# Two alternating sums in DRAM for the first experts' scatter-adds, joined where the projection and the attention load rows

## The reference

```python
x = x + 0.5 * ffn(layernorm(x))
x = x + attn(layernorm(x))
x = x + 0.5 * ffn(layernorm(x))
```

## Time and profile before

| | |
|---|---|
| time, median of 3 runs | 1454.43 us (1454.4 to 1458.55) |
| time of the profiled execution | 1453.73 us |
| its span, first to last instruction | 1452.5 us |
| PE busy | 1225.6 us, 84% |
| DVE busy | 908.8 us, 63% |
| ACT busy | 661.8 us, 46% |
| POOL busy | 531.1 us, 37% |
| mean granted TensorE clock | 0.945 of full speed |
| q0 (software) | 53.49 MB, 18.1% of 16 engines |
| q1 (hardware) | 47.17 MB, 9.4% of 16 engines |

### The profile page before, as it was taken

The page is one execution under the profiler, slowest core; times in us unless marked ns, Lnnn a source line. Parts: engine busy times, 40 slices in busy tenths (PEclk is TensorE's granted clock), DMA queues, the critical chain, the costliest instruction groups (busy, mean ns, idle before and its releaser), DMA issues.

```text
span 1452.5 us, 22060 instructions
## 1 busy us (share of the span) xinstructions
PE 1225.6 (84%) x7484; PEld 781.7 (54%) x7484; DVE 908.8 (63%) x2063; ACT 661.8 (46%) x1313; POOL 531.1 (37%) x423
## 2 busy tenths in 40 slices
PE   3278888865989899999999999999999717998985
PEld 3266666644877554455445455444433316776763
DVE  7865665545999564666576766667620485665653
ACT  2424444432645653555355555455567332443442
POOL 4424444434000110001424553626358362544443
PEclk9689999997999999999999999989999958999998
DMA  9654555443111000000000004010000342555444
GB/s 341 256 167 88 90 97 90 88 71 94 35 32 28 31 31 2 31 31 31 0 31 31 2 1 146 1 59 2 2 30 1 126 174 51 89 94 91 93 88 65
DMA packets 50827, 102.06 MB, mean 70 GB/s; under 512 B 7104, under 2 KB 16576, under 8 KB 50624
## 3 DMA queue, kind: packets, MB, share of 16 engines
q0 software_dynamic: 20928, 53.49, 18.1%
q1 hardware_dynamic: 29792, 47.17, 9.4%
HBM read 67.35 MB, written 38.01 MB: 73 GB/s over the span
## 4 chain that ended last, share of the span: by engine, by line
PE 49%; DMA 25%; DVE 16%; issue 6%; ACT 3%; POOL 0%; SPq 0%; POOLq 0%; DVEq 0%; ACTq 0%
DMA x<-Y,DI 12%; DMA out<-Y,DI 11%; PE bank L1372 9%; PE bank L1384 9%; PE bank L877 8%; PE bank L1397 5%; PE bank L1434 3%; DVE PM L890 3%; PE bank L1202 3%; PE bank L716 2%; DVE bank L892 2%; DMA XG<-xn,TK 2%; PE bank L646 1%; PE bank L739 1%; PE bank L1414 1%
## 5 line engine op out<-in xcount | busy, mean ns | idle before, releaser
L1476 ACT ACTIVATE P<-bank 128x512 f32<-128x512 f32 (+3 forms) x640 | 305.7, 535 | 299.2 <-PE bank L1372 295.3
L890 DVE TENSOR_REDUCE PM<-bank 128x1 f32<-128x512 f32 x384 | 252.8, 685 | 102.2 <-PE bank L877 101.2
L1372 PE MATMUL bank<-Qs,Ks 98*128 98x512 f32 (+3 forms) x640 | 248.3, 412 | 7.9 <-ACT P L1476 6.3
L877 PE MATMUL bank<-Ks,Qs 96*128 96x512 f32 (+3 forms) x640 | 238.1, 391 | 7.3 <-DVE PM L890 4.5
L1372 PEld LDWEIGHTS bank<-Qs,Ks 98*128 98x128 f32 x640 | 117.2, 190 | 151.9 <-issue 85.6
L1515 POOL TENSOR_SCALAR_AFFINE_SELECT P<-P 128x512 f32<-128x512 f32 x64 | 41.2, 644 | 429.3 <-ACT P L1476 290.3
L1530 POOL TENSOR_TENSOR CH<-CH,P 128x512 f32<-128x512 f32 x128 | 160.2, 1281 | 72.3 <-ACT P L1476 71.4
L892 DVE CUSTOM_DVE_ANT_0 bank<-bank,KB 128x128 f32<-128x128 f32 (+3 forms) x256 | 124.8, 497 | 57.9 <-PE bank L877 57.1
L877 PEld LDWEIGHTS bank<-Ks,Qs 96*128 96x128 f32 x640 | 121.8, 191 | 60.7 <-DVE PM L890 31.3
L1384 PE MATMUL bank<-P,V 128*32 128x512 f32 (+3 forms) x1280 | 153.4, 551 | 0.2 <-POOL P L1515 0.2
L827 DVE TENSOR_TENSOR DL<-W,DH 128x512 fp32r<-128x512 f32 x152 | 98.3, 688 | 51.4 <-ACT DH L788 51.4
(11 more groups left out here) (167 smaller groups left out, 1893.7 us busy)
## 6 DMA issues: line engine op xcount, KB each, us to landing
xn<-XN SPq DMA_DIRECT2D x8, 1024.0 KB, 7.0
WR<-L_ffn_w POOLq DMA_DIRECT2D x16, 512.0 KB, 13.8
WR<-L_ffn_w SPq DMA_DIRECT2D x16, 512.0 KB, 7.9
W<-L_ffn_w POOLq DMA_DIRECT2D x8, 512.0 KB, 24.0
XA<-x SPq DMA_DIRECT2D x16, 256.0 KB, 2.7
XO<-x SPq DMA_DIRECT2D x4, 1024.0 KB, 5.4
out<-XO SPq DMA_DIRECT2D x4, 1024.0 KB, 4.4
W<-L_ffn_w SPq DMA_DIRECT2D x8, 512.0 KB, 7.4
```

The costliest lines, as they stand in the source:

```text
L877: pe.matmul(bk(g, bank)[:, 0:n], g.Qs[b][0:96, G % 4 * 4 + h, c * P:c * P + P], g.Ks[0:96, G % 4, k * BQ:k * BQ + n], start=True, stop=Tru ...
L890: dve.tensor_reduce(dst, bk(g, bank)[:, 0:n], AX.X, ALU.max).then_inc(s(f"free{bank}"), 1)
L1372: pe.matmul(bk(g, i % 3)[:, o:BQ], g.Ks[0:98, G % 4, k * P:k * P + P], g.Qs[G // 4][0:98, G % 4 * 4 + j, o:BQ], start=True, stop=True).the ...
L1476: act.activation(a.P4[buffer_of(n)][:, j, o:BQ], bk(g, i % 3)[:, o:BQ], ACT.Exp, scale=scale).then_inc(s("exp"), 1)
```

## The change

The first experts get a second sum, `x1b`, filled with zeros; even tiles add into `x1` and odd tiles into `x1b`. A scatter-add waits for the one two tiles before it instead of the one before. The readers of the sum load the rows of `x1` as before, and POOL then issues a DMA with accumulation that adds the rows of `x1b` on top in SBUF. For the second experts the list of sums has one member, so their waits are those of before. The core of the diff:

```diff
+def added(g, f, j):
+    n = len(g.acc[f])
+    return g.s(f"add{f}_{j % n}"), 16 * (j // n + 1)
+
+def all_added(g, f, wait):
+    for j in range(NJ - len(g.acc[f]), NJ):
+        wait(*added(g, f, j))
...
             pool.wait_ge(s("y"), b + j)
-            if j == 1:
-                before_adding()
+            if j - 1 < len(acc):
+                before_adding(j - 1)
             else:
-                pool.wait_ge(s(f"add{f}"), 16 * (j - 1))
+                pool.wait_ge(*added(g, f, j - 1 - len(acc)))
             pool.indirect_dma_start(
-                out=acc[:, :], ...
+                out=acc[(j - 1) % len(acc)][:, :], ...
...
     def weigh(j):
         if j >= 3:
-            dve.wait_ge(s(f"add{f}"), 16 * (j - 2))
+            dve.wait_ge(*added(g, f, j - 3))
...
 def sp_start_sums(g):
     for q in range(4):
-        sp.dma_start(g.x1[512 * q:512 * q + 512, :], x[512 * q:512 * q + 512, :]).then_inc(s("acc"), 16)
-    sp.dma_start(g.x1[T:T + P, :], zero).then_inc(s("dump"), 16)
+        sp.dma_start(g.x1[512 * q:512 * q + 512, :], x[512 * q:512 * q + 512, :]).then_inc(s("acc0"), 16)
+    sp.dma_start(g.x1[T:T + P, :], zero).then_inc(s("acc0"), 16)
+    for q in range(4):
+        sp.dma_start(g.x1b[512 * q:512 * q + 512, :].rearrange("(i p) d -> i p d", p=P),
+                     zero.unsqueeze(0).to_broadcast([4, P, D])).then_inc(s("acc1"), 16)
+    sp.dma_start(g.x1b[T:T + P, :], zero).then_inc(s("acc1"), 16)
     sp.dma_start(g.out[T:T + P, :], zero).then_inc(s("dump"), 16)
...
 def pool_project(g):
+    def second(i):
+        pool.wait_ge(s(f"xa{i % 3}"), 16 * (i // 3 + 1))
+        pool.dma_start(p.X[:, i % 3, :], g.x1b[i * P:i * P + P, :], accum_op=ALU.add).then_inc(s(f"xb{i % 3}"), 16)
+
+    for i in range(3):
+        second(i)
     pool.memset(g.Ks[96:98, :, :].bitcast(F32), 1.0).then_inc(s("kone"), 1)
...
+    for i in range(3, NT):
+        second(i)
...
     def norm(i):
-        dve.wait_ge(s(f"xa{b}"), 16 * (i // 3 + 1))
+        dve.wait_ge(s(f"xb{b}"), 16 * (i // 3 + 1))
...
-                        put(at + 6, ("xo", G0 // 4))
+                        put(at + 2, ("xo", G0 // 4))
+                        put(at + 7, ("xob", G0 // 4))
                         put(at + 9, ("finish", G0 // 4))
...
+        elif step[0] == "xob":
+            b = step[1]
+            pool.wait_ge(s("xo"), 16 * b + 16)
+            pool.dma_start(a.XO[:], g.x1b[BQ * b:BQ * b + BQ, :].rearrange("(i p) d -> p i d", p=P),
+                           accum_op=ALU.add).then_inc(s("xob"), 16)
...
         if c == 0:
-            dve.wait_ge(s("xo"), 16 * b + 16)
+            dve.wait_ge(s("xob"), 16 * b + 16)
...
+        def sum_started(j):
+            pool.wait_ge(s(f"acc{j}"), 80)
```

More of the change, by code:

```diff
@@ L648, in pe_route, with pool_experts @@
     ins.then_inc(s(f"slots{f}"), 1)
-def pool_experts(g, f, acc, before_adding):
+def added(g, f, j):
[4 more added lines that the diff above has]
+        wait(*added(g, f, j))
+def pool_experts(g, f, before_adding):
     s, pool, r, x = g.s, g.nc.gpsimd, g.r[f], g.x[f]
-    b = f * NJ
+    b, acc = f * NJ, g.acc[f]
     def gather(j):
@@ L675, in pool_experts @@
             pool.wait_ge(s("y"), b + j)
-            if j == 1:
-                before_adding()
+            if j - 1 < len(acc):
+                before_adding(j - 1)
             else:
-                pool.wait_ge(s(f"add{f}"), 16 * (j - 1))
+                pool.wait_ge(*added(g, f, j - 1 - len(acc)))
             pool.indirect_dma_start(
-                out=acc[:, :], out_offset=bass.IndirectOffsetOnAxis(ap=r.DI[:, j - 1:j], axis=0),
-                in_=x.Y[:, (j - 1) % 3, :], in_offset=None, compute_op=ALU.add).then_inc(s(f"add{f}"), 16)
+                out=acc[(j - 1) % len(acc)][:, :], out_offset=bass.IndirectOffsetOnAxis(ap=r.DI[:, j - 1:j], axis=0),
+                in_=x.Y[:, (j - 1) % 3, :], in_offset=None, compute_op=ALU.add).then_inc(added(g, f, j - 1)[0], 16)
 def pe_experts(g, f):
@@ L1001, in sp_project @@
     s, sp, d, p = g.s, g.nc.sync, g.d, g.p
-    sp.wait_ge(s("add0"), 16 * NJ)
+    all_added(g, 0, sp.wait_ge)
     def load(i):
@@ L1022, in pool_project @@
     s, pool, p = g.s, g.nc.gpsimd, g.p
-    pool.wait_ge(s("add0"), 16 * NJ)
+    all_added(g, 0, pool.wait_ge)
+    def second(i):
[3 more added lines that the diff above has]
+        second(i)
     pool.memset(g.Ks[96:98, :, :].bitcast(F32), 1.0).then_inc(s("kone"), 1)
@@ L1037, in dve_project @@
     hd = lambda ap: ap.rearrange("p (h d) -> p h d", d=HD)
-    dve.wait_ge(s("add0"), 16 * NJ)
+    all_added(g, 0, dve.wait_ge)
     def norm(i):
         b = i % 3
-        dve.wait_ge(s(f"xa{b}"), 16 * (i // 3 + 1))
+        dve.wait_ge(s(f"xb{b}"), 16 * (i // 3 + 1))
         dve.bn_stats(p.st[:], p.X[:, b, :]).then_inc(dv.sem, 1)
@@ L1106, in act_project @@
     act.activation(g.NM[:, 0:1], g.Kc[:, C_ID:C_ID + 1], ACT.Sqrt)
-    act.wait_ge(s("add0"), 16 * NJ)
+    all_added(g, 0, act.wait_ge)
     def root(i):
@@ L1331, in attend_plan @@
     assert not later and not extra and not ahead, (later, extra, len(ahead))
-    plan += [("weigh", len(TILES) - 1), ("out", 15), ("xo", 3), ("up1", 4), ("tsum", 15), ("even", 15)]
+    plan += [("weigh", len(TILES) - 1), ("out", 15), ("xo", 3), ("xob", 3), ("up1", 4), ("tsum", 15), ("even", 15)]
     for c in range(6):
@@ L1552, in add, with proj_added @@
         if c == 0:
-            dve.wait_ge(s("xo"), 16 * b + 16)
+            dve.wait_ge(s("xob"), 16 * b + 16)
         dve.tensor_tensor(a.XO[:, c, :], bk(g, bank), a.XO[:, c, :], ALU.add).then_inc(s(f"free{bank}"), 1)
-    def added(b, c):
+    def proj_added(b, c):
         bank, use = g.ring.where[("proj", b, c)]
@@ L1595, in dve_attend @@
         elif kind == "stats":
-            added(step[1], step[2])
+            proj_added(step[1], step[2])
             dve_stats(g, g.R1, a.XO, step[2])
@@ L1604, in dve_attend @@
             c = step[1]
-            added(3, c)
+            proj_added(3, c)
             dve_stats(g, g.R1, a.XO, c)
@@ L1673, in build @@
         g.x1 = nc.dram_tensor("x1", [T + P, D], F32, kind="Internal").ap()
+        g.x1b = nc.dram_tensor("x1b", [T + P, D], F32, kind="Internal").ap()
+        g.acc = [(g.x1, g.x1b), (out,)]
         g.md = [nc.dram_tensor(f"top_{G}", [8, BQ], F32, kind="Internal").ap() for G in range(4 * NB)]
@@ L1705, in build @@
         sp_start_sums(g)
[L1707 to L1711, removed]
+        def sum_started(j):
+            pool.wait_ge(s(f"acc{j}"), 80)
+        pool_experts(g, 0, sum_started)
         pe_experts(g, 0)
@@ L1717, in build @@
         pool_project(g)
-        pe.wait_ge(s("add0"), 16 * NJ)
+        all_added(g, 0, pe.wait_ge)
         pe_project(g)
@@ L1739, in build, with residual_stored @@
         sp_down1(g)
-        def residual_stored():
+        def residual_stored(j):
             pool.wait_ge(s("stored"), 64)
-        pool_experts(g, 1, out, residual_stored)
+            pool.wait_ge(s("dump"), 16)
+        pool_experts(g, 1, residual_stored)
         pe_experts(g, 1)
@@ L1747, in build @@
         dve_experts(g, 1)
-        sp.wait_ge(s("add1"), 16 * NJ)
+        all_added(g, 1, sp.wait_ge)
 def consts():
```

## The result

| | before | after |
|---|---|---|
| median | 1454.41 us (4 runs, 1452.62 to 1458.55) | 1490.8 us (4 runs, 1488.05 to 1493.21) |
| ratio, 95% interval | | 1.0245 (1.0217 to 1.0274) |
| span of the profiled execution | 1452.5 us | 1492.0 us |
| mean granted TensorE clock | 0.945 | 0.928 |
| PE busy | 1225.6 us | 1232.2 us |

A forecast was written before the change was run, and what follows sets the result against it. The prediction took the first experts' serial scatter-adds (5.75 us each) as the bound, PE being capable of 4.82 us a tile. It summed -4.7 (experts) + 17 (projection) + 9 (attention) = +21.3 us, 1476 us, range 1448 to 1497.

The forecast's parts named there:

- The sign: Whole kernel: the change makes it slower, chance 0.82; within 0.03, faster 0.15.
- the forecast: Whole kernel: the main case, +21.3 us to 1476 us, own range 1464 to 1490, chance 0.58.
- dear loads: Projection and attention, rival: accumulating loads cost as much as a scatter-add, 35 and 14 us, whole 1499 us; chance 0.12.
- Part 1: First experts' loop: without the wait for the direct predecessor, PE becomes the bound at 4.82 us a tile.
- Part 2: Fill of x1b: on 4 engines it takes 42 us, ends at 149, leaving the first experts a 4.7 us gain.
- Part 3: Projection: a second DMA in series with each row load costs 17 us together (11 to 36).
- Later tiles: Projection: cycle of load, second load, norm and rotary step becomes 9.65 us, losing 8.7 and 2.2 us.
- First tiles: Projection's start: second loads ahead of POOL's Ks fill delay the weights' split and tile 3, losing 6.2 us.
- Part 4: Attention: the 1 MB second load of XO takes 10 us and costs 9 us together (3 to 15).
- The 4 us for a contest with the weights of the second experts: Attention, block 3: XO's second load meets 4 MB of weights starting on SP's queue, so 4 us were added.
- The fill on 16 engines: Fill of x1b, rival: it ends at 118, gaining 37 us; whole -11, 1443 us; chance 0.16.
- the turning point given: Fill of x1b: the sign turns at a gain of 26 us, a fill ending by 129, on some seven engines or more.

The follow-up runs named there:

- e3: The changed kernel without the second loads of the projection, the odd tiles' sum left out of q, k and v: 1453.7 us, ratio 1.0038 to the kernel before.
- e8: e1 with POOL's setting of Ks and ones moved behind the weights' split and all second loads: 1454.11 us, ratio 1.008 to the kernel before.
- e5: e1 with the projection's second load reading plain rows of x1, without accumulation: 1442.93 us, one run.
- e4: The changed kernel without the accumulating load of the attention's residual (XO): 1483.65 us, ratio 1.0242 to the kernel before.
- e13: e1 run again in another job: 1455.08 us, ratio 1.007 to the kernel before.
- e12: e1 without the second load of the attention's residual (XO): 1451.96 us, ratio 1.0047 to the kernel before.
- e1: The changed kernel with the x1b fill written with outer dimension 128 instead of 4 (16 engines): 1459.7 us, ratio 1.0077 to the kernel before.
- e11: e7 with joins from tile 6 on paced by rotary steps and Ks set behind all joins: 1435.15 us, ratio 0.9929 to the kernel before.
- e7: e1 with POOL adding x1b to x1 in DRAM, 128 rows at a time, instead of any second loads: 1433.39 us, ratio 0.9927 to the kernel before.

## Why the prediction was right, and where it was off

The sign is right, and 1490.8 us lies in the range (1448 to 1497), but 0.8 above the upper end of the forecast's own (1464 to 1490). 15 us were missing. In the profiled spans it is 39.5 against 21.3: 4.8 too little for the experts and 18 for the projection, 6 too much for the attention, and 1.4 behind it. So the misses cancelled in part, and the range held the time because its upper end made room for dear loads, which are not what came; that much is luck. Point by point, against -4.7, +17 and +9:

**Part 1, PE becomes the bound: right.** PE is busy 39.98 of 40 us, and the tile takes 4.92 us, 0.10 above the 4.82 taken from three tiles. Over 32 tiles that is 3.2 us.

**Part 2, the fill on four engines: right in mechanism.** Predicted to end at 149 with scatter-add 1 at 149.8; measured 151.57. The fills ran one behind the other: the chain has four waits of SP and DMA from 95.28 on (14.05, 11.99, 10.13 and 19.22 us). PE's restart at 157.76 was predicted at 156.0. These 1.8 us and the 3.2 above are why the sum is complete at 333.19 and not at 328.4: **0 gained in place of 4.7.** The rule of the Trainium skill that the prediction cites (page "DMA: Bandwidth & Descriptors", section "Why a DMA increments its semaphore by 16 and not by 1"), that the engines used follow the size of the slowest dimension, agrees with the runs with 4, 8 and 128 above.

**Part 3, the projection: right in mechanism, too small in size; this is the term of the sum that failed.** 35.0 us in place of 17.
- Later tiles: a cycle of 2.7 + 4.2 + 2.74 = 9.65 us was worked out, 3.06 + 4.54 + 2.78 = 10.38 was measured, 8 us over eleven cycles. The second load alone was right (4.2 us, median 4.2) and so was DVE's part. The first term left out POOL's wake (0.3 us) and that single row loads took up to 3.4. The second took the statistics to start when the second load lands; in four cycles they started behind score maxima on DVE. The working also kept every later step at its speed of before, while the granted clock fell to 0.93. What the clock alone cost was not measured: e3, without second loads, is back at a clock of 1.00 and at a cycle of 8.69, but that removes both.
- First tiles: 15.9 us in place of 6.2. The working put the fill of `Ks` behind the third row load and priced the weights' split behind it. What came, from the timelines: DVE's first statistics start 12.2 us behind the first row load in place of 2.8, which is 9.4 us, because the first second load is issued 1.4 us after its row load has landed and takes 7.99 us, not 4.2. DVE's first scaling then falls onto the memset and waits for its end (5.67 us in place of 2.07), another 3.6; and tile 3, the first of the later cycle, adds 2.7. e8 shows that moving the memset takes some 6 us off the stretch. The 7.99 us are not the adding: in e5 a plain load at the same place took 6.8. Beside it run two row loads and the 1.5 MB of q, k and v weights, and in 337:345 the DMA share is 0.93 (279 GB/s); it was not tried without the weights, so that cause is argued.

**Part 4, the attention: 9 predicted, about 3 measured.** From the last XA load to block 3's first XO add are 693.4 us against 690.4. The XO adds wait for the second load by 4.86, 5.24 and 5.99 us in blocks 1 to 3, where they waited 2.66, 2.55 and 3.27 before (the first and the last in the earlier trace rows). So they are late by 2.2, 2.7 and 2.7. The row of block 3, after:

```profile
1182.65 0.69 DVE L1585 TENSOR_TENSOR XO<-bank,XO 128x512 f32<-128x512 f32 x1 [5.99 <-DMA XO<-x1b]
```

The load lands after 9.6 us (10 taken). The 4 us for a contest with the weights of the second experts in block 3 did not come: there the wait grew by no more than in block 2. Over eight profiled executions with this add the stretch took 693.4 to 697.0 us, over six without it 688.6 to 692.9 (last column of the table); between single pairs the difference is 2.5 us (after and e4) to 5.4 (e13 and e12), and it is 3 us in the times of e13 and e12, while e4's ratio shows none.

**The rivals.** The fill on 16 engines was forecast to save 37 us there and 11 in all. The experiment with it saved 28, and the whole was 11 us slower than before. The 9 missing are the cadence (3.2) and a fill that held scatter-add 1 for 14.3 us and not 9; and the cost behind it was 33 + 3, not 26. So the turning point given, a fill that ends by 129, was wrong: e1's scatter-add 1 starts at 120.73 and the kernel is still slower. That comes from Part 3; with its 17 us in place of 33 e1 would have been some 5 us faster than the kernel before, by this sum. Dear loads (1499) and the forecast (1476) frame the result. The projection's cost is that of the dear case (35), the attention's is not (3 against 14), and the reason is another: the accumulating load itself landed as forecast, and what surrounds it cost more.

## What to carry to other kernels

Splitting a serial chain of accumulating DMAs over two destinations takes the wait out of the loop, but the join has to be paid: put it where it can run ahead (here in DRAM, outside the cycle of the row buffers: 0.993 of before, out of 0.983 for the loop with no join at all) and not as a second load in series inside a cycle whose slack is smaller than its landing. Count a serial step from row to row (landing, wake, issue, and what the waiting engine has to finish first), and not as the median landing alone, and look at the granted clock of an engine that the new wait leaves idle. Write a fill on SP's queue with its 128 rows, and not the 4 blocks, as the outer dimension, and look at what a moved POOL instruction then overlaps on DVE.

## What the runs showed of the hardware

- A DMA on SP's queue from a DRAM constant to DRAM went at the rate of 4, 8 or up to 16 engines as its outer dimension was 4, 8 or 128: 42.0, 21.9 and 14.3 us for the 4.2 MB, waits of the first scatter-add included. SP's queue itself stood for 37.05 + 10.10 us while it issued the four fills and the dump rows of `x1b` behind them where the fills had an outer dimension of 4, against 13.90 + 2.89 where they had 128. The next DMA on it, the zeros for the dump rows of `out`, was issued at 141.72 and in e1 at 108.15.
- An accumulating DMA of 256 KB into SBUF from POOL's queue lands after 3.9 (e1, e8) to 4.2 us (the change) in the median, a plain one after 2.9 (e5); its issue takes 0.85 us against 0.54. One of 1 MB lands after 9.6 us. From DRAM into DRAM, 256 KB land after 4.9 us (e11, paced) to 6.8 (e7, close behind each other).
- POOL's memset of 2 partitions x 8192 floats (6.92 us) holds up DVE's scaling of 128 x 512 floats from SBUF to SBUF until its end plus 0.27 to 0.29 us, in the twelve traces where they overlap; otherwise it takes 0.55 us. DVE's statistics under the same memset in the kernel before were not lengthened (0.69 us at 335.84, as everywhere).
- PE's granted clock was lower in the runs in which PE waited more often inside the projection's eleven later cycles: 1.00 before and in e3, 0.93 in the change and in e1, 0.97 in e5 and e8. In the cycle from 395.35 PE was busy 0.09 of 2 us in 403:405, and in 407:409 it was granted 0.50.
